# Weights' parts and first blocks made ready a stage ahead, in shared places, at both seams of the MLP

## The reference

```python
h = layer_norm(x) * scale + offset
q, k, v = h @ wq / sqrt(d), h @ wk, h @ wv          # 16 heads of 32, q and k turned
y = softmax(q k^T) v
x = x + y @ wo
x = x + gelu(layer_norm(x, mlp_ln_scale) @ w1) @ w2

att = exp((x @ attention_weights - max) * temperature)
cumv = cumsum(x @ values, axis=1)
attn_out = att * cumv / (att * counts + EPS_ATT)
op = attn_out @ operator + vector
res = relu(concat(x, op) @ ff1 + ff1_bias) @ ff2 + ff2_bias + x
out = layer_norm(res) * ln_gamma + ln_beta
```

## Time and profile before

| | us |
|---|---|
| median of three runs | 3582.47 (3579.41 to 3586.3) |
| the profiled execution | 3573.79 |
| its span | 3572.0 |
| TensorE busy in the span | 3420.8 (96%) |
| VectorE, ScalarE, GpSimd busy | 2079.4, 1508.5, 2016.5 |
| TensorE busy from 2060 to 2115 (seam of attention and MLP) | 19.39 of 55 |
| TensorE busy from 2957 to 3079 (seam of MLP and averages) | 76.28 of 122 |

### The profile page before, as it was taken

How to read it: one execution, slowest core, us unless ns; L and a number is a source line. 1 busy time by engine, 2 the same in 40 slices (tenths; PEclk the granted TensorE clock), 3 DMA queues, 4 the chain that set the end, 5 groups by cost and what they waited for, 6 DMA issues and landing times. The chain is left out here.

```text
span 3572.0 us, 47047 instructions
## 1 busy us (share of the span) xinstructions
PE 3420.8 (96%) x16632; PEld 2230.6 (62%) x16632; DVE 2079.4 (58%) x3331; ACT 1508.5 (42%) x2785; POOL 2016.5 (56%) x1613
## 2 busy tenths in 40 slices
PE   6999899999999999999999959999999995999998
PEld 5777455454554555545455348888888883778877
DVE  6776677777777777777777344222222213454554
ACT  2332466666666666666666632111111112222221
POOL 3644488887978888797888812222222223343342
PEclk9999999999999999999999979999999997999999
DMA  5556677869678686867865543122222114222221
GB/s 193 177 169 205 118 154 138 148 129 154 140 131 152 127 156 133 151 142 132 156 127 107 113 140 107 55 73 75 73 67 75 54 36 139 83 86 76 73 87 41
DMA packets 176737, 419.32 MB, mean 117 GB/s; under 512 B 15382, under 2 KB 62998, under 8 KB 151670
## 3 DMA queue, kind: packets, MB, share of 16 engines
q1 hardware_dynamic: 153606, 249.59, 26.4%
q0 software_dynamic: 22896, 166.73, 24.0%
HBM read 162.25 MB, written 87.03 MB: 70 GB/s over the span
## 5 line engine op out<-in xcount | busy, mean ns | idle before, releaser
L868 DVE TENSOR_REDUCE part_max<-ps_att 128x1 f32<-128x512 f32 x1972 | 1225.4, 683 | 372.2 <-PE ps_att L786 372.1
L914 ACT ACTIVATE probs<-ps_att 128x512 f32<-128x512 f32 x2048 | 1061.7, 603 | 521.9 <-PE ps_att L758 458.7
L965 POOL TENSOR_TENSOR prob_sums<-prob_sums,probs 128x512 f32<-128x512 f32 x884 | 1142.8, 1537 | 60.8 <-DMA probs<-probs 60.8
L810 PE MATMUL ps_att<-probs,v_tok 128*32 128x512 f32 x4096 | 548.3, 607 | 3.1 <-DMA v_tok<-v 3.1
L1456 POOL TENSOR_TENSOR ff_g_lo<-ff_g,ff_g_hi 128x512 fp32r<-128x512 f32 x128 | 164.7, 1287 | 551.5 <-DVE ff_g_hi L1417 551.5
L758 PE MATMUL ps_att<-q_stack,k_stack 97*128 97x512 f32 x768 | 319.8, 424 | 9.9 <-ACT probs L914 9.7
L758 PE MATMUL ps_att<-q_stack,k_first 97*128 97x512 f32 x768 | 324.7, 423 | 2.6 <-ACT probs L914 2.6
L1325 ACT ACTIVATE ff_g<-ps_ff 128x512 f32<-128x512 f32 x128 | 76.5, 597 | 582.2 <-PE ps_ff L1209 582.2
L786 PE MATMUL ps_att<-k_stack,q_stack 96*128 96x512 f32 x768 | 303.8, 396 | 0.0
L786 PE MATMUL ps_att<-k_first,q_stack 96*128 96x512 f32 x756 | 301.9, 399 | 0.0
L1946 POOL TENSOR_TENSOR av_gated_lo<-av_full,av_gated_hi 128x512 fp32r<-128x512 f32 x64 | 94.4, 1475 | 313.9 <-ACT av_gated_hi L1783 313.9
(11 more groups left out here) (209 smaller groups left out, 5514.9 us busy)
## 6 DMA issues: line engine op xcount, KB each, us to landing
probs<-probs POOLq DMA_DIRECT2D x159, 1024.0 KB, 8.6
q_stack<-qk SPq DMA_DIRECT2D x144, 128.0 KB, 6.9
...
k_stack<-qk SPq DMA_DIRECT2D x24, 512.0 KB, 10.4
...
x_in_sb<-in_x SPq DMA_DIRECT2D x8, 1024.0 KB, 6.7
```

Source lines behind the costliest of these rows:

```text
L810: mm = nc.tensor.matmul(o_ps[rows, :], t["v"][:, steps[w]["b"], k, rows], t["p"][:, w % PR, h, :], start=(k == 0), stop=(k == LT - 1))
L868: nc.vector.tensor_reduce(t["pm"][:, r, k:k + 1], mx[mx_uses % 3], AX.X, ALU.max)\
L914: nc.scalar.activation(t["p"][:, at % PR, h, :], sT[(at * G + h) % 3], ACT.Exp)\
L965: nc.gpsimd.tensor_tensor(x, first, t["p"][:, w % PR, h, :], ALU.add).then_inc(s["acc_done"], 1)
```

## The change

- `k_first` and `q_first` have 128 partitions instead of 97 and are kept for all stages; a tensor `rows` is kept for the MLP and the last stage. In the MLP `k_first` holds wo's high and low parts and the high and low parts of h; `q_first` holds those of g. In the last stage `k_first` holds ff1's parts and zT's, `q_first` the gated rows', and `rows` is one of the two zT buffers.
- `prepare` copies wo to a scratch tensor in DRAM. In attention's last unit wo is loaded from it to `k_first` (w = 2), split by ScalarE (after steps 8 to 11) and VectorE (after its last maxima); then y of block 0 (w = 52) and its reciprocal rows (w = 54, four loads of 128x512) are loaded there. The sums' load and reciprocal come six steps sooner.
- The MLP's start has no wo parts and no `load_first`. The first w1 parts are split at m = 12 to 15 of turn -1, the first w2 parts at turn 0's first step, all further ones one step later than before.
- In the MLP's last turn ff1's first half is loaded to `rows` and split into wo's place, and then zT of block 0 is loaded and split into h's place, after the last gelu.
- The last stage starts without these loads and splits. Values come in two halves by columns (heads 0 to 3, 4 to 7). SyncE loads parts 0 to 2 (both halves of values, the first of wp) at once, then stores the gate, then issues three gate rows, then parts 3 and 4 (second of wp, ff2). VectorE makes the running sums of block 0 ahead of the gate and the first low part inside it; GpSimd makes the low parts of parts 2 to 4. In block 0 a gated product follows its value product by three instead of one.

The diff, cut to its core:

```diff
@@ attend, SyncE
-                if at == end - 18:
+                if unit == UNITS - 1 and w == 2:
+                    sp.dma_start(wo_raw.bitcast(F32), a["wo_copy"].rearrange("p k n -> p (k n)")).then_inc(s["wo_in"], 16)
+                if unit == UNITS - 1 and w == 40:
...
+                if unit == UNITS - 1 and w == 52:
+                    sp.wait_ge(s["wo_lo"], DC)
+                    sp.wait_ge(s["y_stored"], 16 * ((UNITS - 2) * NB + 1))
+                    sp.dma_start(y_raw.bitcast(F32).rearrange("p (k t) -> p k t", k=DC),
+                                 a["yT"].rearrange("(k p) t -> p k t", p=P)[:, :, 0:TB]).then_inc(s["first_in"], 16)
+                if unit == UNITS - 1 and w == 54:
+                    sp.wait_ge(s["rl_stored"], 16)
+                    for f in range(DC):
+                        src = a["rl"][f * G:(f + 1) * G, 0:TB].unsqueeze(1).broadcast_to([G, KD, TB])
+                        sp.dma_start(y_rl[:, f * TB:(f + 1) * TB].bitcast(F32), src).then_inc(s["first_in"], 16)
@@ attend, VectorE
+                if at >= end - 17 and at < end - 17 + DC:
+                    i = at - (end - 17)
+                    dve.wait_ge(s["wo_hi"], i + 1)
...
@@ attend, ScalarE
                 exps(at, range(G))
+                if st["unit"] == UNITS - 1 and 8 <= st["w"] < 8 + DC:
...
+                    nc.scalar.activation(wo_hi[:, cols], wo_raw[:, cols].bitcast(F32), ACT.Copy).then_inc(s["wo_hi"], 1)
@@ feed_forward
             if n == -1:
-                return [m] if 4 <= m < WOUT + 2 * WQ else []
-            first = WOUT + 2 * WQ + 2 * m
+                return [WOUT + m - (MC - WQ)] if m >= MC - WQ else []
+            if n == 0 and m == 0:
+                return list(range(WOUT + WQ, WOUT + 2 * WQ))
+            first = WOUT + 2 * WQ + 2 * (m - 1)
...
-                for i in range(4):
-                    load_chunk(i)
-                load_first(0)
                 load_x(0)
-                load_first(1)
-                for i in range(4, 8):
+                for i in range(WOUT, WOUT + 4):
                     load_chunk(i)
...
+                        if n == NA - 1 and m == 1:
+                            sp.wait_ge(s["tb"], TT * NA)
+                            sp.dma_start(x[:], a["ff1"][:, 0:DC, :]).then_inc(s["next_in"], 16)
+                        if n == NA - 1 and m == 9:
+                            sp.wait_ge(s["next_lo"], DC)
+                            sp.wait_ge(s["zf_stored"], 16 * TT)
+                            sp.dma_start(x[:], a["zT"][:, :, 0:TB].rearrange("f p t -> p f t")).then_inc(s["nextz_in"], 16)
@@ average
-        parts = ((a["ff1"], fh, fl, slice(0, 4)), (a["values"], vh, vl, slice(0, 2)), (a["values"], vh, vl, slice(2, 4)),
-                 (a["wp"], wh, wl, slice(0, 4)), (a["wp"], wh, wl, slice(4, 8)), (a["ff2"], eh, el, slice(0, 4)))
+        parts = ((a["values"], vh, vl, slice(0, 4), whole), (a["values"], vh, vl, slice(0, 4), slice(D, 2 * D)),
+                 (a["wp"], wh, wl, slice(0, 4), whole), (a["wp"], wh, wl, slice(4, 8), whole),
+                 (a["ff2"], eh, el, slice(0, 4), whole))
...
-        LOW_POOL, PARTS_AT, SUMS_DVE = 3, HC - DC - 1, (0, 1)
+        LOW_POOL, PARTS_AT, SUMS_DVE = 2, HC - DC - 1, (0, 1)
@@ average, SyncE
-                load_zT(0)
-                load_weight(FF1)
...
-                for i in range(1, 5):
+                for i in range(3):
                     load_weight(i)
                 sp.wait_ge(s["gate"], 1)
...
-                load_weight(FF2)
                 sp.wait_ge(s["gate_stored"], 16 * B)
                 for v in range(3):
                     load_gate(v)
+                for i in range(3, len(weights)):
+                    load_weight(i)
@@ average, TensorE
+                        lag = 3 if n == 0 else 1
                         for h in range(1, HC):
                             values(n, h)
-                            gated(n, h - 1)
-                        gated(n, HC - 1)
+                            if h >= lag:
+                                gated(n, h - lag)
+                        for h in range(HC - lag, HC):
+                            gated(n, h)
@@ average, VectorE
+                for f in range(DC - 1):
+                    running_sum(0, f)
                 dve.wait_ge(s["lg_in"], 16 * (2 * B + 2))
...
-                for f in range(DC):
-                    zT_lo(0, f)
-                weight_lo(FF1)
+                running_sum(0, DC - 1)
...
                 nc.vector.reciprocal(cnt, cnt).then_inc(s["rec"], 1)
+                weight_lo(0)
                 dve.wait_ge(s["rec"], 1)
                 nc.vector.tensor_tensor(lg, lg, cnt, ALU.mult).then_inc(s["gate"], 1)
-                for f in range(DC):
-                    running_sum(0, f)
-                for i in range(1, LOW_POOL):
-                    weight_lo(i)
+                weight_lo(1)
```

172 lines of the change are left out of this document (91 added, 81 removed).

## The result

The changed kernel took 3549.05 us (median of 4 runs, 3540.98 to 3556.93), the kernel before 3582.08 (median of 4, 3579.41 to 3586.3): ratio 0.9913, 95% interval 0.9894 to 0.9931. That is 33.0 us less (the interval gives 25 to 38) where 26.1 were forecast, and 3549 lies inside the range of 3543 to 3567. But it lies in the middle of the range by luck: the terms at both seams were too large, and some 18 us that no term held made up for them.

A forecast was written before the change was run, and what follows sets the result against it. TensorE was taken as full in the MLP, with time to win only at two seams where it idles, 81 us. Terms 20.7 - 1.6 + 7.0 = 26.1 us off 3582.5 gave 3556, range 3543 to 3567.

The forecast's parts named there:

- Seam 1: Between attention and MLP: with projection inputs already in SBUF, the MLP's first up-projection starts 20.7 us earlier.
- some 33 us: Sign expected in the new profile: up-projection some 33 us after attention's last matmul instead of 55.
- seam 2 chain: Last stage's start: gate, its store, gate rows, weight parts 3 and 4, then first gated low part, 4.7 us later.
- first: Rival at seam 2: gate rows don't hold weight parts 3 and 4; win 18.6 instead of 7.0 us; chance 0.14.
- second: Rival at seam 1: the clock stays low through the projections; chance 0.12.
- fourth rival: MLP's first block waits for weight parts, making the kernel slower: 3592 at 3 us per step; chance 0.03.
- Attention's tail: Attention's end: y and reciprocal-row loads beside GpSimd's DMA additions cost 0, bounds 0 and 5 us.
- four subtractions on VectorE ... I price them at nothing: Attention's last unit: four added casts and four subtractions cost nothing; without cover 2.5 us.
- third rival: Attention pays: row loads hold GpSimd's DMA additions 10.4 us, 5.4 paid at attention's end, 3561; chance 0.09.
- The w2 parts: MLP's first block: four w2 parts made after the first gelu delay the first down-projection by 1.6 us, bounds 0 and 3.
- Seam 2, 7.0 forecast: From the MLP's end through block 0 of the last stage: 7.0 us saved, bounds 3 and 18.6.
- 11 groups of 12 (2.8 each): Last stage, block 0: matmuls left after the first gated low part, 30.8 us, besides 10 at half clock, 4.3.

The follow-up runs named there:

- e2: Changed kernel with attention's four reciprocal-row loads issued ahead of the 1 MB load of y instead of behind it; 3542.08 us, ratio 0.9891.
- e1: Changed kernel with the last stage's weight parts 3 and 4 issued ahead of the gate's rows; 3532.73 us, ratio 0.9865.
- e3: Kernel before with only declarations reordered: the MLP's h and g declared first, at low SBUF addresses; 3564.44 us, ratio 0.9949.
- e5: Kernel before with one unused 32-byte tensor behind ln_scale, so MLP operands begin at 32 modulo 64 bytes; 3578.47 us, ratio 0.9973.
- e6: Kernel before with two unused 32-byte tensors, so MLP operands begin at 0 modulo 64 bytes; 3576.03 us, ratio 0.9979.
- e11: Changed kernel with parts 3 and 4 before gate rows, reciprocal rows before y, first w2 parts cast before block 0's up-projections; 3526.38 us, ratio 0.9842.
- e7: Changed kernel with the lag of gated products in the last stage's block 0 put back from three to one; 3552.48 us, ratio 0.9896.
- e4: Changed kernel unchanged, run again for a second profile; 3546.69 us, ratio 0.9899 to the kernel before.

## Why the prediction came out

**Right.** Seam 1's order of events and, but for attention's tail, its length (55.65 less 20.7 is 35.0 us; e2, without the tail's wait, has 35.5; the "some 33 us" among the signs doesn't follow from the sum); the clock coming back in the first projection; no starving of the MLP's steps; both ends of the seam 2 chain up to the first gated low part, within 1 us; parts 3 and 4 held by two engines' gate rows (e1, a DMA share of 0.13). The first, second and fourth rival fell. The second would have cost 6.9 us: 12 matmuls take 5.1 at half clock and 2.8 at full, in three projections; the clock was at 1.00 before the second projection began.

**Attention's tail, priced at 0 of "0 and 5": 2.5 us.** The step that failed is "four subtractions on VectorE ... I price them at nothing". They cost TensorE nothing there, but two lasted 16 us beside GpSimd, SyncE waited for them, and the row loads behind slid to attention's end. The third rival named those loads and their 10.4 us, but the wrong victim: GpSimd's wait of 6.17 was covered, the store of sums was not. In the 16.57 us of the last one GpSimd made three rounds of four additions, and the subtraction ended only as GpSimd paused. I should have weighed it where I had read "1.2 beside GpSimd": the low parts of w1 and w2 in the profile of before take 0.67 to 0.75 us without GpSimd beside them, and eight of the eleven that have it beside them take 1.43 to 1.82.

**The w2 parts, 1.6 forecast: 3.5, and 4.5 with a fall of the clock that came in three of eight profiles; 0.9 less net of the up-product that comes later without them.** The wait was forecast (1.9 to 2.2 measured), and so was the 10 us from the first up- to the first down-product (10.1 to 10.5). The term was mis-sized because it took the 8.4 us of one profile as what that distance had been. Three others with the kernel before's order there (e3, e5, e6) have 7.2 to 7.3, and e11 7.6; in the profile of before the clock came back later, 0.74 over the 5 us before the down-product where those three have 0.87 to 0.89.

**"Work that is only moved inside it costs nothing as long as nothing waits there".** This sentence on the MLP left no room for a gain without a wait. The change moved operands to other places, and e3 shows 18.8 us for that; less 3.5 to 4.5 for the w2 parts, that is about the 13.8 and 15.2 of the table.

**Seam 2, 7.0 forecast (its own figures give 7.3): 2.7 and 4.3 in two profiles.** "11 groups of 12 (2.8 each)" took the groups as free of waits. The last gated group waited 1.8 us, because VectorE feeds one gated product per 5.65 us there, in one of two profiles with half clock behind it. The lag's 5.6 us were real (e7 has two groups more to do and takes their time), and this wait and the clock took back 3.9 of them in the first profile and 1.4 in e4; it is one shortfall, not two. The rest is the chain before, late by 0.7 us and by 1.6.

Together: 20.7 became 18.2 (17.5 in e4), -1.6 became -3.5 to -4.5, 7.0 became 2.7 to 4.3, and 18.8 that were not forecast came from the place of operands. That the time lies inside the range is owed to the last: the three terms of the forecast come to 16 to 18 us, which alone give 3564 to 3566, and the measured time plus 18.8 is 3568, where the range ends at 3567. The way (faster) was forecast rightly; the size was luck. (The chances of "faster" add up to 0.95, not 0.94.)
